# Attention heads beside a recurrence: one head a step where a unit of four was handled at once

## The chip, the cores and the metric

The kernel runs on one core of one Trainium2 chip. The metric is the device time of one execution in microseconds (us), the median of three runs. A core has TensorE (PE in the profile, its weight loads PEld), VectorE (DVE), ScalarE (ACT), GpSimd (POOL) and SyncE (SP), which issues the DMAs. Each engine works through its own list of instructions in order, and waits on semaphores that others raise.

## The reference

A decoder layer in float32 on 1024 rows of width 128. First come four sLSTM layers over 256 positions of 4 sequences. Each step of such a layer needs the state of the step before:

```python
raw = wx_t + jnp.einsum('bhd,hdgo->bhgo', h, rk) + b
mn = jnp.maximum(ir, lfm)
cn = fg * c + ig * jnp.tanh(zr)
nn = fg * n + ig
hn = jax.nn.sigmoid(og) * cn / nn
```

Each layer adds a feed-forward part, and layer norms follow. Then comes cross attention of 16 heads of 64 channels, from the 1024 rows to a context of 6404 rows of width 96: `softmax(q k^T / 8) v`, projected by Wo. Last come a layer norm, eight experts of which every token takes one, and a layer norm.

## The kernel before

**The recurrence.** `slstm_stage` runs the four layers as a wavefront: 38 chunks of 32 steps (`CH` = 32), 1216 steps in all. In a step, PE multiplies the state `st` by 16 recurrent matrices (L1325). ACT takes four activations of the sum, `tf`, `ei`, `tz`, `to` (L1176 to L1179). DVE makes the new state with nine short instructions, `uu` (L1478) first, then `rn`, `vv`, `ww`, `cn`, `hb`, and last the two parts of `st` (L1504, L1507); ACT copies a third part (L1185). PE may then start the next step. The position of a step in its chunk is called t below; at fixed t the engines also do the layers' other work (norms, convolution, gates, feed-forward), in the functions named `beside`.

**Plain chunks.** In the first 10 chunks the engines also prepare keys and values (`ByHead`: one tile of 512 columns at each t of its `PLACES`, copied by ACT at L1195) and fused weights (`WeightsByHead`). ACT scales six tiles of the context at t = `T_SCALE` (L1216), writes queries' weights at t = `T_QUERY` with two copies (L1223), and converts `wv_sb` once, in chunk 0 at t = `T_PARTS` (L1219); DVE makes the remainder of that one step later (L1523).

**Units.** In the other 28 chunks (896 steps) the attention of the first 512 rows runs beside the recurrence. A unit is 4 heads of one block of 128 rows; there are 16 units. Unit u starts at step 64 + 52 u (steps are counted from the first of the 28 chunks here). In each of its first 51 steps PE makes a tile of scores for 4 heads (L133, L135), ACT takes the exponential (L1165), and one step later PE multiplies by the values into `OA` (L1273). In the 52nd step there are no scores, and ACT copies `OA` to `o_sb` (L1169).

**Work around a unit.** Before a unit starts, its queries and, for each row, an upper value of its scores must be there. `Timetable` gives each piece its step:
- `queries`: PE multiplies `xat` by `qk_w` for 4 heads into one bank (L184), ACT copies it as two halves in the next two steps (L1145). For units from 2 on this is the last step of a unit.
- `head_queries`: the same with `wq_d`, 3 steps later (L192); ACT copies two halves (L1152), DVE subtracts and writes the low part 2 steps after (`dve_q_low`, L197).
- `maxes`: 52 pairs per unit, 13 pieces of keys by 4 heads. PE makes one piece of scores (`pe_max_score`, L144), DVE reduces it to its maximum (`dve_max`, L152). They are spread over the window of steps before the unit by the room on DVE: `ROOM` less `vector_load` at that t, less `special`.
- `column` and `row`: 4 and 3 steps before the unit, DVE reduces the 13 maxima of each head (L156), PE turns the 4 columns into rows (L162), ACT copies them (L1157).
- `out`: in the first step of the next unit, PE makes the 4 denominators (`pe_den`, L169), DVE takes the reciprocal (L1418), then PE projects 4 heads (`pe_project`, L176) and DVE adds them up (`dve_heads_out`, L207, L210).

**Two banks.** All these use two PSUM banks, `MB[0]` and `MB[1]`. `take` hands the bank that is read first to the next user, by the order of the steps; before PE writes a bank, `bank_for` waits until its last reader is done:

```python
def bank_for(key):
    bank, n = plan.uses[key]
    if n:
        pe.wait_ge(mb_read[bank], n)
```

**Order in a step.** PE: 16 recurrent matmuls, scores, values, bank work (`bank_work`: out, turn, queries, head queries, row, maxima), then `beside`. ACT: four activations, `beside_early`, `unit_early` (copies out of banks), the copy to `st`, `unit_late` (the exponential). DVE: the nine state instructions, `beside`, `unit_work` (block steps, out, low part, maxima, column).

After the recurrence, `attention_tail` does the other 512 rows and then the experts run; of these the change touches nothing that is computed.

## Time and profile before

| | |
|---|---|
| median of 3 runs | 4360.94 us (4358.36 to 4362.44) |
| the profiled execution | 4370.43 us |
| its span, first to last instruction | 4368.7 us |
| PE, DVE, ACT, POOL busy | 85%, 82%, 65%, 24% |
| recurrence, plain chunks | 56.9 to 867.5 us |
| recurrence, 28 chunks with units | 867.5 to 3225.9 us |
| tail and experts | 3225.9 to 4368.7 us |

PEclk, in 40 slices of the span: `6555555556999999999999999999978999999998`. A digit is the granted clock of TensorE in tenths of its full speed; the two levels are 1.0 (2.4 GHz) and 0.5 (1.2 GHz). A row of the windows view gives the busy time of each engine in a stretch with its number of instructions, and the mean granted clock. In the timeline a row gives the start, the duration, the engine, the line, what is written from what, how many instructions are merged, and in brackets how long the engine sat idle before it and what released it.

### The profile page before, as it was taken

Reading aid. Unit: us, or ns where it says so; the run is one execution under the profiler, and the core shown is the slowest. Engines: PE = TensorE matmul, PEld = TensorE weight load, DVE = VectorE, ACT = ScalarE, POOL = GpSimd, SP = SyncE. Lnnn points to the kernel's source line nnn. Section 1 sums busy time; section 2 is a strip of 40 time slices with the busy share of each in tenths; the row PEclk is TensorE's granted clock in tenths of the full one; section 3 lists DMA queues with packets and bytes.
Section 4 is the critical chain, followed back from the end, with each engine's and each line's share of the span. In section 5 each row is a group of like instructions: output and inputs, shape, how many; then the busy total and the mean of one; then the engine's idle time right before and its main releaser. Section 6 shows DMA issues by size and latency. Waiting matters only on the chain. (4 is left out here: it accounts for less than half of the span.)

```text
span 4368.7 us, 114098 instructions
## 1 busy us (share of the span) xinstructions
PE 3717.4 (85%) x42154; PEld 2230.8 (51%) x42154; DVE 3571.7 (82%) x16022; ACT 2839.8 (65%) x9118; POOL 1037.4 (24%) x1217
## 2 busy tenths in 40 slices
PE   5777777647998999999999999999868999999987
PEld 3433433434555555555555555555534555556555
DVE  7887788777888888888888888888758888888875
ACT  4555555544666666666666666666645888888884
POOL 1000000000000000000000000000005888889983
PEclk6555555556999999999999999999978999999998
DMA  3222222201333243343333333333333133322300
GB/s 100 67 68 70 66 70 71 75 16 24 74 81 76 66 89 73 73 88 72 70 81 73 78 70 81 80 73 83 80 87 93 48 78 78 78 55 63 78 25 25
DMA packets 262091, 305.39 MB, mean 70 GB/s; under 512 B 21752, under 2 KB 255032, under 8 KB 256376
## 3 DMA queue, kind: packets, MB, share of 16 engines
q1 hardware_dynamic: 258356, 293.73, 28.1%
q8 instruction: 332, 5.44, 0.6%
q10 hardware_dynamic: 3176, 4.36, 0.4%
q14 instruction: 227, 1.86, 0.2%
HBM read 241.03 MB, written 55.78 MB: 68 GB/s over the span
## 5 line engine op out<-in xcount | busy, mean ns | idle before, releaser
L1325 PEld LDWEIGHTS G<-st,rec_w 128*128 128x128 f16 x19456 | 604.2, 99 | 981.7 <-DVE st L1507 946.1
L1325 PE MATMUL G<-st,rec_w 128*128 128x1 f16 x19456 | 685.2, 165 | 354.9 <-DVE st L1507 341.0
L1779 POOL TENSOR_TENSOR plt<-pft,pht 128x512 f16<-128x512 f32 x765 | 867.2, 1166 | 156.0 <-DVE pht L2022 83.4
L1273 PE MATMUL OA<-pf,vals 128*97 128x512 f32 (+1 forms) x1632 | 877.7, 620 | 1.1
L1185 ACT ACTIVATE st<-hb 32x16 f16<-32x16 f32 x1216 | 258.8, 213 | 695.6 <-DVE hb L1502 695.2
L152 DVE TENSOR_REDUCE mx<-MB 128x1 f32<-128x512 f32 (+1 forms) x832 | 538.5, 661 | 56.2 <-PE MB L144 48.0
L1165 ACT ACTIVATE pf<-SC,ln_prob 128x512 f32<-128x512 f32 (+1 forms) x816 | 560.9, 687 | 20.5
L152 DVE TENSOR_REDUCE mx<-MT 128x1 f32<-128x512 f32 (+1 forms) x832 | 523.0, 663 | 54.1 <-PE MT L1828 44.1
L1774 ACT ACTIVATE pft<-ST,ln_prob 128x512 f32<-128x512 f32 (+1 forms) x816 | 537.4, 689 | 34.9 <-PE ST L1850 34.4
L1772 ACT ACTIVATE pht<-ST,ln_prob 128x512 f16<-128x512 f32 x510 | 351.5, 689 | 197.1 <-PE ST L1850 192.6
L135 PE MATMUL SC<-q_in,k_in 65*128 65x128 f16 (+1 forms) x3264 | 476.5, 223 | 0.0
L133 PE MATMUL SC<-qd_in,kc_in 128*128 128x128 f16 (+1 forms) x3264 | 472.1, 221 | 0.0
L1176 ACT ACTIVATE tf<-G 32x16 f32<-32x16 f32 x1216 | 213.0, 175 | 332.1 <-PE G L1325 301.6
L1478 DVE SCALAR_TENSOR_TENSOR uu<-tf,cn 32x32 f32<-32x32 f32 x1216 | 213.7, 176 | 236.0 <-ACT tf L1176 227.5
L769 POOL TENSOR_SCALAR vare<-yvar 128x4 f32<-128x4 f32 x39 | 7.6, 194 | 1550.3 <-DVE yvar L881 1550.3
L1912 PEld LDWEIGHTS OT<-vc,pht 128*128 128x128 f16 (+1 forms) x3264 | 251.4, 98 | 215.6 <-issue 17.3
L777 POOL TENSOR_SCALAR vare<-mv 128x1 f32<-128x1 f32 x78 | 15.0, 192 | 1393.6 <-DVE mv L787 1393.6
L1828 PE MATMUL MT<-kc,qd 128*128 128x512 f16 (+1 forms) x832 | 306.2, 389 | 43.0 <-DVE mx L152 41.0
L144 PE MATMUL MB<-keys_h,qh 96*128 96x512 f16 (+1 forms) x832 | 308.0, 394 | 31.4 <-DVE mx L152 28.3
L1912 PE MATMUL OT<-vc,pht 128*128 128x129 f16 (+1 forms) x3264 | 321.4, 221 | 9.9 <-DVE o_n L1978 6.6
L1484 DVE RECIPROCAL rn<-cn 32x16 f32<-32x16 f32 x1216 | 293.1, 241 | 41.9
L135 PEld LDWEIGHTS SC<-q_in,k_in 65*128 65x128 f16 (+1 forms) x3264 | 321.6, 99 | 0.0
(362 smaller groups left out, 7118.7 us busy)
## 6 DMA issues: line engine op xcount, KB each, us to landing
kc_in<-scr_k SPq DMA_DIRECT2D x384, 256.0 KB, 4.3
k_in<-scr_k SPq DMA_DIRECT2D x192, 256.0 KB, 4.9
vc<-scr_v SPq DMA_DIRECT2D x16, 1644.8 KB, 15.6
kc<-scr_k SPq DMA_DIRECT2D x32, 816.0 KB, 12.2
scr_v<-v_hl SPq DMA_DIRECT2D x24, 1032.0 KB, 5.5
scr_k<-k_hl SPq DMA_DIRECT2D x192, 128.0 KB, 1.7
k<-scr_k SPq DMA_DIRECT2D x16, 816.0 KB, 6.6
kc_in<-scr_k SPq DMA_DIRECT2D x32, 192.0 KB, 3.6
```

The costliest lines, as they stand in the source:

```text
L133: pe.matmul(bank[0:k, cols], at.kc_in[:, kept, i, first:first + k], at.qd_in[:, unit, cols], start=(i == 0), stop=False, skip_group_check= ...
L135: mm = pe.matmul(bank[0:k, cols], at.k2_in[:, kept, i, first:first + k], at.q2_in[:, unit, cols], start=False, stop=True, skip_group_check ...
L144: return pe.matmul(bank[:, 0:a1 - a0], at.qh[0:at.DC, unit, i * P:(i + 1) * P], at.keys_h[0:at.DC, a0:a1], start=True, stop=True)
L152: return at.nc.vector.tensor_reduce(at.mx[:, i, c:c + 1], bank[:, 0:a1 - a0], AX_X, ALU.max)
L1165: s.activation(pf[0:rows, tile % 2, :], SC[tile % 2][0:rows, :], ACT.Exp, scale=1.0 / at.S_SCALE, bias=at.ln_prob[0:rows, 0:1]).then_inc(p ...
L1273: pe.matmul(OA[0:at.DC + 1, :], at.vals[0:rows, i, :], pf[0:rows, tile % 2, :], start=(i == 0), stop=(i == KT - 1)).then_inc(pv_done, 1)
L1325: mm = pe.matmul(g[:, t, c:c + 1], rec_w[:, c, :], st[:, c:c + 1], start=False, stop=(c == C - 1), skip_group_check=True)
L1772: s.activation(ph[0:k, t % NP_, :], SC[t % NS][0:k, :], ACT.Exp, scale=1.0 / at.S_SCALE, bias=at.ln_prob[0:k, 0:1])
L1774: s.activation(pf[0:k, t % NP_, :], SC[t % NS][0:k, :], ACT.Exp, scale=1.0 / at.S_SCALE, bias=at.ln_prob[0:k, 0:1]).then_inc(p_done, 1)
L1779: return eng.tensor_tensor(pl[0:k, t % NP_, :], pf[0:k, t % NP_, :], ph[0:k, t % NP_, :], ALU.subtract)
L1828: pe.matmul(MB[done % 2][:, 0:a1 - a0], qd[:, h % NK_, i * P:(i + 1) * P], kc[:, h % NK_, a0:a1], start=True, stop=True).then_inc(m_done, 1)
L1912: pe.matmul(OA[i // 2][:, (i % 2) * 256:(i % 2) * 256 + VC], ph[0:k, t % NP_, i * P:(i + 1) * P], vc[0:k, g % 2, j, :], start=(j == 0 and ...
```

## The change

Queries, head queries, rows of maxima and the projection are done by single heads, one head in a step, each with a bank of its own. There are now 64 `queries`, 64 `head_queries`, 64 `column`, 64 `row` and 60 `out` steps, where there were 16, 16, 16, 16 and 15. A step takes at most one of `queries`, `head_queries`, `row`, `turn` and `out` (the set `taken`), `queries` and the head queries inside units only at t in `FOR_QUERIES`, `out` only at t in `FOR_OUT`. In a taken step at most one maximum is made, elsewhere at most four, but for the last step of a window. DVE reads `out` and head queries one step after PE, ACT copies queries, head queries and rows one step after PE. In the plain chunks `T_SCALE`, `T_QUERY` and `T_PARTS` move. The matmul for the denominator goes into column 128 of the bank that gets the projection of the same head. `tile_scores` waits at a unit's start for four banks of each kind in place of one, and the first piece of each head waits for that head's queries. The tail's own column of maxima keeps its old form. The core of the diff:

```diff
-def dve_max_column(at):
-    return at.nc.vector.tensor_reduce(at.mxn[:, :], at.mx[:, :, :], AX_X, ALU.max)
-def pe_max_row(pe, at, bank):
-    for i in range(at.HEADS_A_UNIT):
-        mm = pe.matmul(bank[at.DHEAD:at.DHEAD + 1, i * P:(i + 1) * P], at.mxn[:, i:i + 1], at.identa[:, :], start=True, stop=True)
-    return mm
+def dve_max_column(at, i):
+    return at.nc.vector.tensor_reduce(at.mxn[:, i:i + 1], at.mx[:, i, :], AX_X, ALU.max)
+def pe_max_row(pe, at, bank, i):
+    return pe.matmul(bank[at.DHEAD:at.DHEAD + 1, 0:P], at.mxn[:, i:i + 1], at.identa[:, :], start=True, stop=True)
 
...
-def pe_queries(pe, at, bank, unit):
-    for i in range(at.HEADS_A_UNIT):
-        mm = pe.matmul(bank[0:at.DC, i * P:(i + 1) * P], at.qk_w[:, unit * at.HEADS_A_UNIT + i, :], at.xat[:, :],
-                       start=True, stop=True)
-    return mm
...
+def pe_out(pe, at, bank, unit, i):
+    cols = slice(i * P, (i + 1) * P)
+    pe.matmul(bank[:, P:P + 1], at.o_sb[:, cols], at.pick_den[:, :], start=True, stop=True)
+    return pe.matmul(bank[:, 0:P], at.o_sb[0:at.DC, cols], at.vo_w[:, unit * at.HEADS_A_UNIT + i, :], start=True, stop=True)
+def pe_queries(pe, at, bank, unit, i):
+    return pe.matmul(bank[0:at.DC, 0:P], at.qk_w[:, unit * at.HEADS_A_UNIT + i, :], at.xat[:, :], start=True, stop=True)
...
+    FOR_QUERIES = (0, 1, 2, 3, 5, 6, 7, 11, 12, 15, 18, 19, 20)
+    FOR_OUT = (1, 2, 4, 7, 8, 14, 15, 18, 21, 27, 31)
...
-        self.out = {start[u] + period: u for u in range(units - 1)}
...
-        self.queries = {35: 0, 46: 1}
-        self.queries.update({start[v - 2] - 1: v for v in range(2, units)})
-        self.head_queries = {s + 3: v for s, v in self.queries.items()}
-        self.column = {start[v] - 4: v for v in range(units)}
-        self.row = {start[v] - 3: v for v in range(units)}
-        asked = {v: s for s, v in self.queries.items()}
-        special = {s: 1.3 for s in self.out}
-        special.update({s: 0.6 for s in self.column})
+        H = range(at.HEADS_A_UNIT)
+        taken = set(self.turn)
+        def next_free(places, s):
+            while s % chunk_steps not in places or s in taken:
+                s += 1
+            taken.add(s)
+            return s
+        self.queries, self.head_queries, self.out, self.column, self.row = {}, {}, {}, {}, {}
+        asked = {}
+        asked[0] = 34
+        for i in H:
+            self.queries[next_free(range(chunk_steps), 34 + i)] = 0, i
+        for i in H:
+            self.head_queries[next_free(range(chunk_steps), 40 + 5 * i)] = 0, i
+        for i in H:
+            s = next_free(self.FOR_QUERIES, start[0] + 1 + i)
+            self.queries[s] = 1, i
+            asked.setdefault(1, s)
+        for i in H:
+            self.head_queries[next_free(range(chunk_steps), start[0] + 22 + 5 * i)] = 1, i
+        for u in range(units):
+            for i in H:
+                if u:
+                    self.out[next_free(self.FOR_OUT, start[u] + 2 + 10 * i)] = u - 1, i
+            if u + 2 < units:
+                for i in H:
+                    s = next_free(self.FOR_QUERIES, start[u] + 1 + 4 * i)
+                    self.queries[s] = u + 2, i
+                    asked.setdefault(u + 2, s)
+                for i in H:
+                    s = next_free(self.FOR_QUERIES, start[u] + 17 + 5 * i)
+                    assert s < start[u + 1] - 5
+                    self.head_queries[s] = u + 2, i
...
+        special = {s + 1: 0.55 for s in self.out}
-            special[s + 2] = special.get(s + 2, 0.0) + 0.7
+            special[s + 1] = special.get(s + 1, 0.0) + 0.25
...
+                if s != window[-1]:
+                    upto = min(upto, n + (1 if s in taken else 4))
                 if upto > n:
                     self.maxes.setdefault(s, []).extend((v, i) for i in range(n, upto))
                 n = upto
+            for i in H:
+                last = max(s for s in window if (v, (i + 1) * len(at.KEYS) - 1) in self.maxes.get(s, ()))
+                self.column[last + 1] = v, i
+                s = last + 2
+                while s in taken or len(self.maxes.get(s, ())) > 1:
+                    s += 1
+                assert s < start[v] - 1
+                taken.add(s)
+                self.row[s] = v, i
...
-                take(("den", self.out[s]), s + 0.5)
-                take(("out", self.out[s]), s + 0.6)
+                take(("out",) + self.out[s], s + 1.7)
-                take(("queries", self.queries[s]), s + 2.3)
+                take(("queries",) + self.queries[s], s + 1.3)
             if s in self.head_queries:
-                take(("head queries", self.head_queries[s]), s + 2.5)
+                take(("head queries",) + self.head_queries[s], s + 1.7)
             if s in self.row:
-                take(("row", self.row[s]), s + 1.3)
+                take(("row",) + self.row[s], s + 1.3)
...
-    T_SCALE, SCALE_TILES, T_QUERY, T_PARTS = 16, 6, 27, 26
+    T_SCALE, SCALE_TILES, T_QUERY, T_PARTS = 9, 6, 29, 30
...
+                        if step - 1 in plan.queries:
+                            v, i = plan.queries[step - 1]
+                            bank, n = plan.uses["queries", v, i]
+                            a.wait_ge(mb_full[bank], n + 1)
+                            s.activation(at.qh[0:at.DC, v % at.UNITS_A_BLOCK, i * P:(i + 1) * P], MB[bank][0:at.DC, 0:P],
+                                         ACT.Copy).then_inc(mb_read[bank], 1)
+                        if step - 1 in plan.head_queries:
+                            v, i = plan.head_queries[step - 1]
+                            bank, n = plan.uses["head queries", v, i]
+                            a.wait_ge(mb_full[bank], n + 1)
+                            s.activation(at.qd_in[:, v % at.UNITS_A_BLOCK, i * P:(i + 1) * P], MB[bank][:, 0:P],
+                                         ACT.Copy).then_inc(hq_hi, 1)
...
-                            u = plan.out[step]
+                            u, i = plan.out[step]
                             pe.wait_ge(o_kept, u + 1)
-                            bank, full = bank_for(("den", u))
-                            pe_den(pe, at, bank).then_inc(full, 1)
-                            bank, full = bank_for(("out", u))
-                            pe_project(pe, at, bank, u % at.UNITS_A_BLOCK).then_inc(full, 1)
+                            bank, full = bank_for(("out", u, i))
+                            pe_out(pe, at, bank, u % at.UNITS_A_BLOCK, i).then_inc(full, 1)
...
-                        if step in plan.out:
-                            u = plan.out[step]
-                            bank, n = plan.uses["den", u]
+                        if step - 1 in plan.out:
+                            u, i = plan.out[step - 1]
+                            done = at.HEADS_A_UNIT * u + i
+                            bank, n = plan.uses["out", u, i]
                             dve.wait_ge(mb_full[bank], n + 1)
-                            v.reciprocal(at.rden[:, :], MB[bank][:, 0:at.HEADS_A_UNIT]).then_inc(mb_read[bank], 1)
-                            dve.wait_ge(mb_read[bank], n + 1)
-                            bank, n = plan.uses["out", u]
-                            dve.wait_ge(mb_full[bank], n + 1)
-                            dve_heads_out(dve, at, MB[bank], at.y_unit[:, u + 1, :], y_step, (at.HEADS_A_UNIT - 1) * u,
-                                          mb_read[bank])
-                        if step - 2 in plan.head_queries:
-                            q = plan.head_queries[step - 2]
-                            bank, n = plan.uses["head queries", q]
-                            dve.wait_ge(hq_hi, 2 * (q + 1))
-                            dve_q_low(at, MB[bank], q % at.UNITS_A_BLOCK).then_inc(mb_read[bank], 1)
+                            v.reciprocal(at.rden[:, i:i + 1], MB[bank][:, P:P + 1]).then_inc(den_ready, 1)
+                            dve.wait_ge(den_ready, done + 1)
+                            y, head = at.y_unit[:, u + 1, :], MB[bank][:, 0:P]
+                            if i == 0:
+                                v.tensor_scalar(y, head, at.rden[:, 0:1], None, ALU.mult).then_inc(mb_read[bank], 1)
+                            else:
+                                last_bank, last = plan.uses["out", u, i - 1]
+                                dve.wait_ge(mb_read[last_bank], last + 1)
+                                v.scalar_tensor_tensor(out=y, in0=head, scalar=at.rden[:, i:i + 1], in1=y,
+                                                       op0=ALU.mult, op1=ALU.add).then_inc(mb_read[bank], 1)
+                        if step - 1 in plan.head_queries:
+                            q, i = plan.head_queries[step - 1]
+                            bank, n = plan.uses["head queries", q, i]
+                            dve.wait_ge(hq_hi, plan.head_queries_done[q, i])
+                            dve_q_low(at, MB[bank], q % at.UNITS_A_BLOCK, i).then_inc(mb_read[bank], 1)
```

## Rows read from the trace of the kernel before

**Rows 1.** Windows: stretch, us, busy (count) of PE, PEld, DVE, ACT, POOL, PEclk, DMA.

```profile
867.50:1054.70 187.20, 98.72 (x1255) 64.35 (x1256) 141.61 (x739) 68.91 (x352) 8.52 (x24) 0.50 0.08 16
1054.70:3225.90 2171.20, 1977.63 (x24423) 1205.03 (x24421) 1840.73 (x9640) 1445.56 (x5352) 95.59 (x272) 0.97 0.36 76
```

**Rows 2.** Timeline of a step with no maximum, from state to state.

```profile
2043.19 0.17 DVE L1507 TENSOR_TENSOR st<-hb,st 32x16 f16<-32x16 f32 x1
...
2043.42 0.55 PE L1325 MATMUL G<-st,rec_w 128*128 128x1 f16 x16 [0.39 <-DVE st L1507]
...
2044.06 0.17 ACT L1176 ACTIVATE tf<-G 32x16 f32<-32x16 f32 x1
...
2044.27 0.18 DVE L1478 SCALAR_TENSOR_TENSOR uu<-tf,cn 32x32 f32<-32x32 f32 x1
...
2045.74 0.55 PE L1325 MATMUL G<-st,rec_w 128*128 128x1 f16 x16 [0.39 <-DVE st L1507]
```

**Rows 3.** Timeline of steps with one maximum and with two.

```profile
1989.88 1.28 DVE L152 TENSOR_REDUCE mx<-MB 128x1 f32<-128x512 f32 x2
...
1990.35 0.17 ACT L1176 ACTIVATE tf<-G 32x16 f32<-32x16 f32 x1
...
1991.08 0.17 DVE L1478 SCALAR_TENSOR_TENSOR uu<-tf,cn 32x32 f32<-32x32 f32 x1
```

**Rows 4.** Timeline, PE's first recurrent matmul after a step with one maximum.

```profile
2048.12 0.55 PE L1325 MATMUL G<-st,rec_w 128*128 128x1 f16 x16 [0.24 <-DVE st L1507]
```

**Rows 5.** Windows: steps 3 to 48 of each unit; the last unit, and the sum.

```profile
3111.10:3218.60 107.50, 95.32 (x1296) 57.75 (x1294) 75.71 (x489) 78.97 (x294) 4.61 (x14) 1.00 0.36 75
sum 1837.80, PE 1663.74 PEld 988.90 DVE 1614.50 ACT 1263.32 POOL 84.03; mean PE 103.98 PEld 61.81 DVE 100.91 ACT 78.96 POOL 5.25
```

**Rows 6.** Windows: the six steps around each of 15 unit ends; two, and the sum.

```profile
1592.30:1610.20 17.90, 17.12 (x214) 11.64 (x212) 14.26 (x73) 11.40 (x43) 0.00 (x0) 1.00 0.07 14
...
2136.30:2162.40 26.10, 25.04 (x211) 18.00 (x209) 14.67 (x71) 10.81 (x39) 0.00 (x0) 0.67 0.17 35
...
sum 314.80, PE 297.42 PEld 205.44 DVE 215.06 ACT 171.93 POOL 11.56; mean PE 19.83 PEld 13.70 DVE 14.34 ACT 11.46 POOL 0.77
```

**Rows 7.** Timeline around the unit end at 2010 us.

```profile
2003.58 0.39 PE L144 MATMUL MB<-keys_h,qh 96*128 96x512 f16 x1 [0.79 <-DVE mx L152]
...
2008.40 1.11 PE L184 MATMUL MB<-xat,qk_w 128*96 128x128 f32 x8
...
2010.61 1.02 PE L169 MATMUL MB<-pick_den,o_sb 97*128 97x1 f32 x8
...
2012.66 2.07 PE L176 MATMUL MB<-vo_w,o_sb 96*128 96x128 f32 x8 [1.03 <-DVE rden L1418]
```

**Rows 8.** Timeline, the rows of another unit at the full clock.

```profile
2277.93 1.03 PE L162 MATMUL MB<-identa,mxn 128*1 128x128 f32 x8
```

**Rows 9.** Groups by line, DVE, 1054.7 to 3225.9: name, shapes, count, busy us, mean ns, idle.

```profile
L210 DVE SCALAR_TENSOR_TENSOR y_unit<-MB,rden,y_unit 128x128 f32<-128x128 f32 x45 | 15.8, 351 | 1.6
...
L197 DVE TENSOR_TENSOR q_in<-MB,qd_in 64x512 f16<-64x512 f32 x14 | 9.4, 668 | 0.1
...
L943 DVE TENSOR_TENSOR x<-TP,x 128x128 f32<-128x128 f32 x26 | 7.6, 292 | 0.8
...
L156 DVE TENSOR_REDUCE mxn<-mx 128x4 f32<-128x52 f32 x15 | 2.9, 194 | 0.4 <-issue 0.3
L1418 DVE RECIPROCAL rden<-MB 128x4 f32<-128x4 f32 x15 | 2.7, 180 | 3.5 <-PE MB L169 3.4
```

**Rows 10.** Timeline of plain steps at t = 16, then t = 27, ScalarE.

```profile
261.70 0.60 ACT L1195 ACTIVATE k_hl<-SC 128x512 f16<-128x512 f32 x1 [0.43 <-DMA scr_k<-k_hl]
262.20 0.68 ACT L1216 ACTIVATE vals<-vals 128x576 f32<-128x576 f32 x1
...
372.14 0.60 ACT L1195 ACTIVATE k_hl<-SC 128x512 f16<-128x512 f32 x1 [1.02 <-PE SC L1345]
...
372.64 0.50 ACT L1223 ACTIVATE wq_d<-wq_sb 128x128 f32<-128x128 f32 x2
```

More of the change, by code:

```diff
@@ L292, in __init__ @@
                 n = upto
+            for i in H:
[7 more added lines that the diff above has]
+                self.row[s] = v, i
+            assert n == at.MX
+        for tile in self.queries.values():
+            asked_at = next(s for s, key in self.queries.items() if key == tile)
+            assert asked_at < min(s for s, keys in self.maxes.items() if (tile[0], tile[1] * len(at.KEYS)) in keys)
         self.uses, free, count = {}, [-1.0, -1.0], [0, 0]
@@ L1256, in tile_scores @@
                             for kind in ("head queries", "row"):
-                                bank, n = plan.uses[kind, u]
-                                pe.wait_ge(mb_read[bank], n + 1)
+                                for head in range(at.HEADS_A_UNIT):
+                                    bank, n = plan.uses[kind, u, head]
+                                    pe.wait_ge(mb_read[bank], n + 1)
                             if u == 0:
@@ L1433, in unit_work @@
                         if step in plan.column:
-                            u = plan.column[step]
+                            u, head = plan.column[step]
                             for bank in range(2):
-                                n = max(n for (kind, *key), (b, n) in plan.uses.items() if kind == "max" and key[0] == u and b == bank)
-                                dve.wait_ge(mb_read[bank], n + 1)
-                            dve_max_column(at).then_inc(m_col, 1)
+                                n = max((n for (kind, *key), (b, n) in plan.uses.items()
+                                         if kind == "max" and key[0] == u and key[1] // len(at.KEYS) == head and b == bank), default=-1)
+                                if n >= 0:
+                                    dve.wait_ge(mb_read[bank], n + 1)
+                            dve_max_column(at, head).then_inc(m_col, 1)
                     def dve_renew(t, c, k):
```

68 lines of the change are left out of this document (27 added, 41 removed).

## The prediction, made before the changed kernel was run

> **What bounds the kernel now.** I read the page first, then windows by stage, then timelines of single steps, and last windows cut at the unit ends. The change touches only the recurrence, 56.9 to 3225.9 us. There no engine's mean load decides, but the loop from state to state. In a step without extras TensorE's recurrent matmuls start at 2043.42 and the next ones at 2045.74: 2.32 us [rows 2]. Two engines can lengthen it. VectorE is done with the state at 2043.19 + 0.17 = 2043.36 and starts `uu` at 2044.27, so what it does in between costs nothing up to 0.91 us. TensorE sits idle for 0.39 us before the next matmuls; with one maximum 0.24 us is left [rows 2, 4]. Two maxima take VectorE 1.28 us, and `uu` starts 0.73 us after `tf` where 0.21 is normal: 0.5 us late [rows 2, 3].
>
> The 832 steps with units take 2171.2 us [rows 1]. At 2.32 each they would take 1930.2; 241 us is excess. The windows divide it. Steps 3 to 48 of all units, 736 steps, take 1837.8 us, 2.50 each [rows 5]. The six steps around each of 15 unit ends, 90 steps, take 314.8 us, 3.50 each [rows 6]. The first 64 steps, in which unit 0 has its 52 maxima squeezed into some 24 steps, take 187.2 us against 148.5 [rows 1]: 39 us excess.
>
> Why a unit end is long: rows of maxima for four heads hold TensorE about 1.0 us, queries about 1.1 [rows 7, 8], in steps whose slack is 0.2 to 0.4. At `out` the projection waits for VectorE's reciprocal, which stands behind the state in VectorE's queue (TensorE idle 1.03 us), and VectorE then needs 4 x 0.351 us [rows 7, 9]. Part of the length is the clock: the end at 1592 has 1.00 throughout and takes 17.9 us, the one at 2136 has a mean of 0.67 and takes 26.1 [rows 6]. A mean of 0.67 is two thirds of the stretch (17.2 us) at 1.2 GHz, and 8.2 us dearer: 0.48 us a us. Over all 15 ends it is about 0.40. The mean of 0.97 over 2171 us [rows 1] is 130 us at the lower level, so some 52 us of time.
>
> **What the change removes.** No unit end has batches of four any more. If its six steps cost what interior steps of units 0 to 14 cost, (1837.8 - 107.5) / 690 = 2.51 us [rows 5], 90 steps take 226 us: 89 us go. But the work comes back elsewhere, and it is priced for all 832 steps at once.
>
> **Maxima by steps.** In the trace before I counted the interior steps by their maxima and read for each the time from state to `uu` beyond 0.91. 155 steps with none are 0.03 us long, 467 with one 0.15, 114 with two 0.45 (half of [rows 3]'s case falls where other VectorE work is small). Check: 5 + 70 + 51 = 126 us, and the windows give 1837.8 - 736 x 2.32 = 130 [rows 5]. Working the new `Timetable` through gives 197 steps with none, 491 with one, 143 with two, one with three: 6 + 74 + 64 + 1 = 145 us.
>
> **What the single heads add.** From the same timetable:
> - TensorE, at full clock, a quarter of the batches: 0.24 to 0.28 for queries, row and denominator, as much for the projection, so about 0.5 for `out` [rows 7, 8]. Beside a maximum, queries and row just fill the 0.24 left: 0.03 each, about 100 steps, 3 us. `out` with a maximum: 52 steps, 0.2 each, 10 us.
> - VectorE for one head of the low part: 64x512 takes 0.668, 128x128 from PSUM 0.292 [rows 9], so 0.29. For one head of `out`: 0.18 + 0.35 and a wait between, 0.58. In steps with one maximum and no bank wait (9 and 16 of them) I take 0.2 and 0.25: 6 us. A column costs about 0.15 (four heads take 0.194), felt in 28 steps with maxima: 4 us.
> - **A new wait.** VectorE reads `out` and the head queries one step after TensorE, so their bank stays held. In 48 of the 832 steps TensorE needs a second bank in just that step (91 has head queries and a maximum, 92 a row and a maximum); before, 20 steps were so. TensorE's maximum then waits behind VectorE's state and its read, and behind it in TensorE's queue stand `beside` and the next recurrent matmuls. VectorE, from the end of the state: read 0.29, semaphore 0.05, the matmul 0.39 [rows 7], maximum 0.66, other work about 0.3: 1.7 against 0.91, some 0.8 long where 0.15 to 0.45 is charged already. I add 0.6: 29 us. Bounds: 0.2 (10 us), if the other work falls into the wait, and 1.0 (48 us) behind an `out`; [rows 7] shows 0.79 us of idle for a wait of this kind.
>
> ScalarE's copies are one of 128 columns in place of two of 256, one step later, and lie in its gap between `to` and the `st` copy; cost 0, and up to 0.1 us in steps where a norm also stands there (at most 10 us in all). The eight waits at a unit's start are for steps at least three earlier. No DMA, and no place in SP's or POOL's list, moves.
>
> Adders: 3 + 10 + 6 + 4 + 29 = 52 us, bounds 30 to 85.
>
> **The clock.** The last step of a unit keeps its missing scores and the first its missing values, so TensorE is still little loaded there, but the long waits are gone. I take half of the 130 us at the lower level, 65 x 0.40 = 26 us; bounds 0 and 52.
>
> So 832 steps: 1930 + 145 + 52 + 26 = 2153 us against 2171: -18. The first 64 steps keep batches of four and five maxima (7 steps with three or more, before 10): -2, bounds -10 and +6.
>
> **The weight copies.** At t = 16 the scale of 0.68 us starts at 262.20, inside the key copy that ends at 262.30, and runs to 262.88, where `tf` follows. Without it `tf` could start 0.58 earlier; 8 chunks: 4.6 us. At t = 27 the key copy ends at 372.74, the two query copies at 373.14: 0.40, 8 chunks, 3.2 us [rows 10]. At t = 9 and 29 no key copy stands in the slot, and in the later chunks the exponentials fit into it. T_PARTS acts once; I take 0 (bounds -1 and +1). Sum -8, bounds -10 and -3.
>
> **Two rules of the Trainium skill.** The 128-wide operation at 0.292 us and the 512-wide one at 0.668 [rows 9] leave 0.17 us that does not depend on width. "VectorE: DVE Perf Modes", section on the TRN2 errata, says that every instruction pays such a fixed part and advises tiles of 512 elements or more, against this change. Ten more VectorE instructions a unit (3 low parts, 3 reciprocals, 3 columns) at about 0.17 would be 25 us if all of it were in the loop. By my sum only what exceeds the 0.91 counts. The granted clock falls at unit ends in which TensorE shows 25.0 us busy of 26.1 [rows 6]. "TensorE: Matmul & The Clock Gate", Part 1, ties the lower level to an idle TensorE; going by idleness alone the time at 1.2 GHz would be gone, which is the rival below.
>
> **Sum.** -18 - 2 - 8 = -28 us on the profiled execution (4370.4 us, span 4368.7). The median of the runs shown is 4360.94, 9 us less; I take the same difference: 4333 us.
>
> **Rivals.**
> - More gain: the clock never falls (-26), or the bank waits hide behind VectorE's other work (-29). Either gives about -55: 4306. For it: four of 15 ends stay at 1.00 already. Against: a unit's last and first step keep their small load.
> - No net change: the clock falls as long as before (+26): -2, 4359. For it: falls come also away from unit ends, after steps with idle TensorE, and 48 bank waits make more such steps.
> - Slower, one mechanism: each bank wait leaves TensorE without work and the clock falls for a step behind it. A step at 1.2 GHz costs 2.5 x 0.48 = 1.2 us; 48 of them are 58, less the 10 taken for falls there already: +48, so +20 and 4381. It decides from 31 of 48 on: 28 + 9 us are needed.
> - The work is not spread: heads crowd in neighbouring steps since the allowed t are few (head queries of unit 4 at 193, 194, 195). It would show as the second rival; its part in the 48 is counted.
>
> **Chances.** Forecast 0.52 (own range 4318 to 4348), more gain 0.22, no net change 0.15, slower 0.11. A measurement can tell 0.2%, 8.7 us. Faster: 0.52 and 0.22, 0.74; within 0.15; slower 0.11. Range 4302 to 4360: it takes in the larger gain and most of the third case.
>
> **What would show it.** Six-step windows around unit ends near 15 to 17 us in place of 21. Interior steps up from 2.50 to about 2.58. TensorE waiting for `q_in` or `y_unit` of VectorE before L144's matmuls, some 48 times. A mean clock of 0.98 or more in the units. In the plain chunks `tf` 0.4 to 0.6 us earlier after t = 16 and 27. Wrong would be: bank waits of over 1.3 us each, interiors above 2.62, a clock at 0.96 or less, or new ScalarE delay of the `st` copy.

## The result, and the profile after

The changed kernel takes 4332.73 us, the median of 5 runs (4330.71 to 4336.2), where the kernel before took 4360.94 (5 runs, 4349.77 to 4362.44): ratio over all runs 0.9949, 95% interval 0.9937 to 0.9960. It is faster by 0.5%; the two medians alone are 28.2 us apart (0.65%). The prediction was 4333 us, with 4302 to 4360 as range.

Windows of the kernel after, columns as in [rows 1]: the plain chunks, the first 64 steps of the others, the steps with units. Before, the last two took 187.20 and 2171.20 us [rows 1].

```profile
56.85:861.90 805.05, 600.32 (x6470) 316.59 (x6468) 645.59 (x3567) 476.62 (x1990) 34.71 (x100) 0.50 0.21 69
861.90:1036.24 174.34, 93.39 (x1226) 58.30 (x1227) 137.55 (x740) 68.96 (x356) 8.42 (x24) 0.50 0.08 17
1036.24:3188.68 2152.44, 1970.13 (x24446) 1208.08 (x24447) 1847.19 (x9769) 1469.86 (x5456) 95.12 (x272) 0.97 0.36 77
```

Both kernels cut at the same events (each step's `tf`) give the table: 37.7 us of span are gone.

| us | before | after | difference | predicted |
|---|---|---|---|---|
| plain chunks | 810.7 | 805.1 | -5.6 | -8 |
| first 64 steps | 187.2 | 174.3 | -12.9 | -2 |
| 831 steps with units | 2168.8 | 2152.4 | -16.4 | -18 |
| tail and experts | 1145.2 | 1142.3 | -2.9 | 0 |

The profiled execution of the kernel before (4370.43 us) is 9.5 us above its median, and that of the kernel after is its median; so the column of differences sums to 37.8 us where the medians differ by 28.2. The tail isn't touched by the change; it spreads over 1141.5 to 1146.2 us in the kernels measured here.

Windows after of six steps around the unit ends (two, and the sum of 15), then of steps 3 to 48 of the units (the last, and the sum), which answer to [rows 5, 6]:

```profile
1571.04:1589.88 18.84, 18.38 (x180) 10.37 (x178) 13.67 (x70) 10.45 (x40) 0.00 (x0) 0.70 0.06 14
...
2927.64:2942.83 15.19, 13.45 (x162) 8.14 (x159) 13.30 (x76) 11.16 (x42) 1.07 (x4) 0.89 0.66 122
...
sum 251.60, PE 234.15 PEld 139.59 DVE 201.97 ACT 159.50 POOL 11.61; mean PE 15.61 PEld 9.31 DVE 13.46 ACT 10.63 POOL 0.77
...
3075.44:3183.80 108.36, 96.70 (x1310) 59.49 (x1308) 77.09 (x497) 79.35 (x294) 4.60 (x14) 1.00 0.34 74
sum 1887.81, PE 1723.70 PEld 1059.42 DVE 1637.82 ACT 1302.05 POOL 83.52; mean PE 107.73 PEld 66.21 DVE 102.36 ACT 81.38 POOL 5.22
```

An end takes 16.8 us in place of 21.0, 63 us less for 15; an interior step takes 1887.8 / 736 = 2.565 in place of 2.497, 50 us more in all. The shortest end has a clock of 0.89 and the longest 0.70: all 15 still lose the clock for a while, where four of 15 did not before.

**The new wait, in a timeline** of the kernel after (start, us, engine, line; in brackets the idle time and its end). Head queries stand in two steps in a row here:

```profile
1123.65 0.16 DVE L1553 TENSOR_TENSOR st<-hb,st 32x16 f16<-32x16 f32 x1
...
1124.12 0.28 DVE L195 TENSOR_TENSOR q_in<-MB,qd_in 64x128 f16<-64x128 f32 x1
...
1124.46 0.39 PE L144 MATMUL MB<-keys_h,qh 96*128 96x512 f16 x1 [0.77 <-DVE q_in L195]
...
1124.69 0.54 PE L1364 MATMUL G<-st,rec_w 128*128 128x1 f16 x16
1124.89 0.69 DVE L152 TENSOR_REDUCE mx<-MB 128x1 f32<-128x512 f32 x1 [0.48 <-PE MB L144]
...
1125.27 0.18 ACT L1216 ACTIVATE tf<-G 32x16 f32<-32x16 f32 x1 [0.78 <-PE G L1364]
...
1125.50 0.17 DVE L1524 SCALAR_TENSOR_TENSOR uu<-tf,cn 32x32 f32<-32x32 f32 x1
```

The state is done at 1123.81, but TensorE's recurrent matmuls start at 1124.69 and not at 1123.87: they stand behind a maximum (L144) that waits for the bank that VectorE's low part (L195) frees at 1124.40. From state to `uu` it is 1.69 us, 0.78 over the floor of 0.91. The groups of the stretch with units count such waits; the first row is of the kernel before, the second of the one after:

```profile
L144 PE MATMUL MB<-keys_h,qh 96*128 96x512 f16 x776 | 275.7, 380 | 5.5 <-DVE mx L152 5.5
```

```profile
L144 PE MATMUL MB<-keys_h,qh 96*128 96x512 f16 x780 | 277.3, 383 | 41.2 <-DVE q_in L195 21.0 <-DVE y_unit L1466 16.0 <-DVE mx L152 4.2
```

**Where the clock falls** in the kernel after, in windows of the first and second step of a unit and the first recurrent matmuls of the second:

```profile
1986.83:1989.46 2.63, 1.49 (x28) 1.17 (x29) 2.42 (x14) 1.61 (x7) 0.00 (x0) 0.74 0.13 21
1989.46:1993.33 3.87, 3.87 (x31) 2.04 (x30) 3.16 (x14) 1.61 (x7) 0.00 (x0) 0.50 0.02 4
```

```profile
1988.81 0.59 PE L1364 MATMUL G<-st,rec_w 128*128 128x1 f16 x16 [1.13 <-DVE st L1553]
...
1990.07 1.97 PE L1314 MATMUL OA<-pf,vals 128*97 128x512 f32 x2
```

The first step of a unit has no values to multiply, and TensorE is idle for 1.13 us of it. Within that idle time its clock goes to 1.2 GHz: the mean granted clock is 0.98 from 1987.50 to 1988.10 and 0.50 from 1988.10 to 1988.80. The values of the second step take 1.97 us, and it takes 3.87 us.

### The profile page after: what moved, and what is told of

It reads as the page before. It is cut to its first block and busy times, and to the rows that moved or that the text cites. A ratio compares the mean times of both kernels' runs of the same rounds, so it can differ in the third digit from the quotient of the medians.

```text
span 4331.0 us, 114618 instructions
## 1 busy us (share of the span) xinstructions
PE 3704.3 (86%) x42154; PEld 2228.9 (51%) x42154; DVE 3573.7 (83%) x16163; ACT 2871.1 (66%) x9230; POOL 1036.1 (24%) x1217
## 5 line engine op out<-in xcount | busy, mean ns | idle before, releaser
L1205 ACT ACTIVATE pf<-SC,ln_prob 128x512 f32<-128x512 f32 (+1 forms) x816 | 562.3, 689 | 20.6
L1958 PEld LDWEIGHTS OT<-vc,pht 128*128 128x128 f16 (+1 forms) x3264 | 251.2, 98 | 215.1 <-issue 16.4
L144 PE MATMUL MB<-keys_h,qh 96*128 96x512 f16 (+1 forms) x832 | 306.7, 396 | 60.3 <-DVE q_in L195 22.9
## 6 DMA issues: line engine op xcount, KB each, us to landing
kc<-scr_k SPq DMA_DIRECT2D x32, 816.0 KB, 12.9
```

The source lines that it names most:

```text
L144: return pe.matmul(bank[:, 0:a1 - a0], at.qh[0:at.DC, unit, i * P:(i + 1) * P], at.keys_h[0:at.DC, a0:a1], start=True, stop=True)
L1205: s.activation(pf[0:rows, tile % 2, :], SC[tile % 2][0:rows, :], ACT.Exp, scale=1.0 / at.S_SCALE, bias=at.ln_prob[0:rows, 0:1]).then_inc(p ...
L1958: pe.matmul(OA[i // 2][:, (i % 2) * 256:(i % 2) * 256 + VC], ph[0:k, t % NP_, i * P:(i + 1) * P], vc[0:k, g % 2, j, :], start=(j == 0 and ...
```

## The experiments

These measures are used in the text. "Low" is TensorE's time at 1.2 GHz in the steps with units. "Full excess" and "low excess" are the sums of the time from state to `uu` beyond 0.91 us, over the steps at the full clock and over those that touch a stretch at the lower one. They come from the profiled execution alone; the ratio comes from 4 to 11 runs and has the last word. "Ends" counts the unit ends, of the 15 six-step windows, with a mean granted clock of 1.00. "Clock" is the mean granted clock of whole executions, the lowest and the highest of that kernel's runs. e1 to e4, e5 to e8 and e9 to e12 are three groups, each with its own runs of the kernel before.

| kernel | ratio to before (95%) | units, us | low | full excess | low excess | ends | clock |
|---|---|---|---|---|---|---|---|
| before | 1 | 2168.8 | 135 | 154.5 | 81.5 | 4 | 0.852 to 0.860 |
| after | 0.9949 (0.9937 to 0.9960) | 2152.4 | 129 | 181.5 | 42.2 | 0 | 0.854 to 0.857 |
| e1 weights only | 0.9987 (0.9977 to 0.9997) | 2161.9 | 114 | 165.5 | 66.6 | 3 | 0.856 to 0.860 |
| e2 no bank wait | 0.9917 (0.9903 to 0.9931) | 2140.9 | 142 | 157.7 | 53.5 | 0 | 0.853 to 0.856 |
| e3 clock filled | 0.9942 (0.9926 to 0.9958) | 2141.4 | 63 | 186.8 | 25.0 | 13 | 0.858 to 0.864 |
| e4 out batch | 0.9965 (0.9952 to 0.9978) | 2158.2 | 147 | 159.1 | 69.2 | 0 | 0.852 to 0.855 |
| e5 changed again | 0.9959 (0.9946 to 0.9971) | 2163.6 | 154 | 178.2 | 56.1 | 0 | 0.852 to 0.855 |
| e6 rows batch | 0.9930 (0.9918 to 0.9942) | 2149.4 | 116 | 178.4 | 41.4 | 0 | 0.856 to 0.859 |
| e7 queries batch | 0.9903 (0.9888 to 0.9919) | 2128.5 | 54 | 178.8 | 20.6 | 8 | 0.863 to 0.864 |
| e8 no wait, filled | 0.9876 (0.9862 to 0.9890) | 2126.8 | 79 | 165.9 | 31.6 | 7 | 0.859 to 0.862 |
| e9 = e7 again | 0.9909 (0.9896 to 0.9923) | 2134.7 | 64 | 176.7 | 26.3 | 9 | 0.860 to 0.862 |
| e10 query batch moved | 0.9967 (0.9954 to 0.9979) | 2162.6 | 132 | 175.1 | 55.7 | 0 | 0.855 to 0.856 |
| e11 out only | 0.9926 (0.9912 to 0.9939) | 2145.9 | 96 | 174.5 | 39.0 | 9 | 0.857 to 0.862 |
| e12 batch, filled | 0.9887 (0.9874 to 0.9901) | 2125.6 | 48 | 172.8 | 20.9 | 11 | 0.862 to 0.866 |

**e1: the weight copies alone** (kernel before otherwise).

```diff
-    T_SCALE, SCALE_TILES, T_QUERY, T_PARTS = 16, 6, 27, 26
+    T_SCALE, SCALE_TILES, T_QUERY, T_PARTS = 9, 6, 29, 30
```

> The kernel before with only the three times of the weight copies moved (t = 16, 27, 26 to 9, 29, 30). Theory (from the changed kernel's plain chunks, 805.1 us against 810.7): the copies' steps win 5.1 us at t = 16, and at t = 27 and 28 together nothing, since TensorE's tile of step 27 is late by its own work; so -5 to -6 us. Rival (my prediction's step): both win, -8 us. A second rival: the plain chunks gain nothing when measured alone, 0 us, and the 5.6 are from elsewhere.

Measured 0.9987, by that ratio 5.7 us less (the medians differ by 4.0); the plain chunks take 805.1 us, as in the kernel after. Step by step, the kernel after against the kernel before (e1 gives the same within 0.2 us): the ten steps t = 16 are 5.1 us shorter, t = 26 0.7, and t = 27 2.35; but t = 28 is 2.75 longer and t = 30 0.4. T_QUERY wins nothing. The timeline after at t = 27 and 28 shows why:

```profile
370.39 0.60 ACT L1235 ACTIVATE k_hl<-SC 128x512 f16<-128x512 f32 x1 [1.02 <-PE SC L1384]
...
371.01 0.18 ACT L1216 ACTIVATE tf<-G 32x16 f32<-32x16 f32 x1
...
372.46 0.16 DVE L1553 TENSOR_TENSOR st<-hb,st 32x16 f16<-32x16 f32 x1
372.54 0.63 PE L1384 MATMUL SC<-keys_h,wk_h 96*128 96x512 f16 x1
...
372.97 0.21 PE L1364 MATMUL G<-st,rec_w 128*128 128x1 f16 x1
```

`tf` follows the key copy at once, as predicted, and the step is 0.38 shorter; the state is done at 372.62. But TensorE, at 1.2 GHz here, is still at its own key tile (L1384) and starts the next step at 372.97, 0.3 late. What one step gains the next one loses.

**e2: the bank waits taken away.** Maxima keep out of the steps in which VectorE reads `out` or head queries, where these would need a second bank; 7 such waits remain, in steps with three or four maxima.

```diff
+        held = {s + 1 for s in (*self.out, *self.head_queries)}
-                    upto = min(upto, n + (1 if s in taken else 4))
+                    upto = min(upto, n + (4 - 3 * (s in taken or s in held) - (s in taken and s in held)))
```

> The changed kernel, but in a step in which VectorE still has to read a projection or head queries at most one maximum is made, and none if that step also holds queries, head queries, a row or a projection. Steps in which TensorE must wait for a bank behind VectorE fall from 48 to 7 of 832; for it, 5 steps get three maxima and 2 get four. Theory: a bank wait costs about 0.7 us more than a plain step with one maximum (measured excess 0.91 against 0.17 to 0.25), so 41 x 0.7 = -29 us, less 10 for the crowded steps: -18 us (-10 to -25) against the changed kernel. Rival: VectorE's own load in these steps is what costs, the wait lies beneath it, and the load only moves: 0 us, up to +5.

0.9917: 14 us less than the change by the ratios (0.9949 - 0.9917 = 0.0032), within the 10 to 25 expected. In its trace the full excess falls from 181.5 to 157.7, 24 us, while low excess rises by 11. The waits are worth that 24 us: 48 of them cost 0.907 us each in the kernel after, 43.5 in all, of which the maxima in those steps would have cost 12 anyway; and seven steps at full clock that now have three or four maxima take 10 us of excess.

**e3: the clock held up at unit ends.** Two matmuls of 512 columns in the last step of a unit and four in the first, whose result nobody reads; what is computed stays as it was.

```diff
+                                for _ in range(n):
+                                    pe.matmul(SC[(tile + (first == 0)) % 2][:, 0:512], at.qh[0:at.DC, u % at.UNITS_A_BLOCK, 0:P],
+                                              at.keys_h[0:at.DC, 0:512], start=True, stop=True)
```

> The changed kernel with 2 more float16 matmuls of 512 columns in the last step of a unit (where scores are missing) and 4 in the first of the next (where values are missing), into a bank of scores that nobody reads; results are unchanged. Theory: TensorE's small load in these two steps is what lets the clock fall at 14 of 15 unit ends; filled, the time at 1.2 GHz in the units falls from 129 us to 40 or less, and at the 0.23 us a us that the changed kernel shows that is -20 us (-12 to -28). Rival 1: the price is the 0.40 of my prediction: -36 us. Rival 2: the falls stem from other steps and stay: 0 us.

The trace has 63 us at the lower level in place of 129, unit ends of 15.5 us (232.3 / 15), and 13 of 15 ends at the full clock where the kernel after has none. The clock is higher in every execution: the six have 0.858 to 0.864, the ten of the changed kernel (with e5) 0.852 to 0.857. But the trace is of the fastest of the six (4324.3); four of them, at 0.858 to 0.860, took 4335.0 to 4342.8, and the median, 4335.2, is not below the change's. The expected 20 us did not come, and the ratio can't tell e3 from the change: that filling lowers the time is not shown by this run. e8 bears on it.

**e4: `out` in one batch again**, the rest as changed.

```diff
-            for i in H:
-                if u:
-                    self.out[next_free(self.FOR_OUT, start[u] + 2 + 10 * i)] = u - 1, i
+        self.out = {start[u] + period: u for u in range(units - 1)}
```

> The changed kernel with denominators and projections as before: four heads at once in the first step of the next unit, DVE reading them in that step. Theory: the unit end waits twice for VectorE there and is dearer by about 35 us over 15 ends, while 52 steps with a head's projection (0.1 each) and 18 held banks (0.7) are saved, about 18: +15 to +22 us against the changed kernel. Rival: the projection's batch was the whole length of the unit ends, since queries and rows fit beside it: +40 us or more.

0.9965, 7 us more than the change; unit ends 278.7 in place of 251.6, interiors 1866.4 in place of 1887.8. That is less than the 15 to 22 us expected, and the two intervals overlap: what `out` by heads is worth beside the other single heads is not shown by this run. e11 says more.

**e5: the changed kernel once more.**

> The changed kernel itself, on the same chip as the other experiments of this call, as the control for their differences. Both theories expect the ratio measured first, 0.9949 (0.9937 to 0.9960), 4336 us; a time outside 4328 to 4344 would say that the differences between calls are larger than the effects of the parts.

4345.07 against 4362.21, ratio 0.9959; so the change is faster again, but by 17 us where it was 28; the time is 12 us above the first one and just outside the 4328 to 4344 that were named. Its trace has 154 us at the lower level where the other had 129, and 14 us more of low excess: the same program loses the clock for different times. That is the size below which differences between groups of runs aren't to be read here.

**e6: columns and rows in batches again**, and **e7: queries and head queries in batches again**, each with the rest as changed, in one group with e5.

```diff
-            for i in H:
-                last = max(s for s in window if (v, (i + 1) * len(at.KEYS) - 1) in self.maxes.get(s, ()))
...
+        self.column = {start[v] - 4: v for v in range(units)}
+        self.row = {start[v] - 3: v for v in range(units)}
```

> The changed kernel with columns and rows of maxima as before: one column reduction 4 steps and four row matmuls 3 steps before a unit. Theory: the batch made step 49 of a unit about 1.0 us long, 15 us in all; spread, rows cost 0.1 in 31 steps, 0.7 in the 7 to 9 with a held bank and columns 0.1 in 28, about 12 us. So +3 us (0 to +8) against the changed kernel: nearly nothing. Rival: the unit ends' gain is shared evenly by the three kinds of batch: +10 to +15 us.

```diff
+        self.queries = {35: 0, 46: 1}
+        self.queries.update({start[v - 2] - 1: v for v in range(2, units)})
+        self.head_queries = {s + 3: v for s, v in self.queries.items()}
```

> The changed kernel with queries and head queries as before: four heads in the last step of a unit and three steps later, two half copies each, VectorE's low part two steps after. Theory: the two batches made steps 51 and 2 long by 12 and 19 us in all and brought some of the first 64 steps' 13 us; spread, 30 bank waits at 0.7 take 21 back. So +8 to +15 us against the changed kernel, part of it in the first 64 steps. Rival: the batches cost more than the spread work in every kind alike: +20 us or more; second rival: the bank waits eat the whole, 0 or less.

e6 is 14 us faster than e5, e7 25 us (0.9903 against 0.9959), where both were expected to be slower. I had held that batches cost; that fell. e6's gain lies in the low excess (41.4 in place of 56.1), with the full excess the same; its interval overlaps that of the first measurement of the change. The batch takes 40 of the 48 bank waits with it (8 are left), and yet the full excess is the same as e5's, 178.8 against 178.2: the batches cost at full clock about what the waits did. What differs is the lower clock: 54 us in place of 154, low excess 20.6 in place of 56.1. Two theories were left: fewer waits, or the batch's place, the last step of a unit, in which scores are missing.

**e8: e2 and e3 together** (its diff is the two).

> Both edits at once: no bank waits (4321 us measured alone, 15 us below the changed kernel) and the filled steps at the unit ends (in its profiled execution 11 us below the changed kernel in the units, in the median of its runs nothing). Theory: the fills win what the clock costs at unit ends, some 0.17 to 0.23 us a us, but runs differ by when the clock falls, so a median of 4310 to 4320. Rival: filling wins nothing that lasts, 4321 or above.

0.9876, 4306.97 us: 38 us below e5 in the same group, and against the change 26 by the medians and 32 by the ratios; the fastest kernel here, faster than e2 and e3, and below the 4310 to 4320 expected. Full excess 165.9, low excess 31.6. From e2 it differs by the filled matmuls alone: the ratio falls from 0.9917 to 0.9876, 18 us, with intervals that don't overlap, though the two were measured in different groups; the ends at the full clock go from none to 7 and the low excess from 53.5 to 31.6. This is the best evidence here that filling lowers the time.

**e9 and e10: the batch's place.** e9 is e7 again; e10 moves one number.

> The kernel with queries and head queries in batches of four and all else as changed, once more, as the base of this group. Ratio to before 0.990 as measured (0.9888 to 0.9919); TensorE at 1.2 GHz in the units for 45 to 75 us.

```diff
-        self.queries.update({start[v - 2] - 1: v for v in range(2, units)})
+        self.queries.update({start[v - 2] + 2: v for v in range(2, units)})
```

> One number differs from the base of this group: the batch of queries stands in a unit's third step in place of its last one (the head queries three steps behind it as before). Theory: what made the batch cheap is that it gives TensorE work in the step without scores, so that the clock doesn't fall at the unit end. Then the time at 1.2 GHz goes from 50 us back to 100 to 140, and the kernel is 15 to 30 us slower than the base (steps with a bank wait go from 8 to 19, of which 7 us). Rival: the gain came from the 40 bank waits that are gone; then the time at 1.2 GHz stays at 45 to 75 us and the kernel is 5 to 10 us slower than the base.

e10 is 25 us slower than e9 (4350.32 against 4325.58) and all of it is the clock: low 132 in place of 64, low excess 55.7 in place of 26.3, full excess unchanged, no end at the full clock in place of 9, and 0.855 or 0.856 in all five executions against 0.860 to 0.862 in e9's four. The same unit end in windows of single steps, the last step of a unit, the first and the second, with the recurrent matmuls that end the idle time of the first; e9, then e10:

```profile
1984.58:1987.25 2.67, 2.67 (x31) 1.75 (x31) 2.23 (x12) 1.82 (x7) 0.00 (x0) 1.00 1.04 208
1987.25:1989.58 2.33, 1.40 (x29) 1.01 (x27) 2.12 (x13) 1.99 (x7) 0.00 (x0) 1.00 0.00 0
1989.58:1992.24 2.66, 2.36 (x31) 1.27 (x29) 2.45 (x14) 1.99 (x7) 0.00 (x0) 1.00 0.00 0
```

```profile
1988.94 0.55 PE L1351 MATMUL G<-st,rec_w 128*128 128x1 f16 x16 [0.93 <-DVE st L1542]
```

```profile
1994.20:1996.47 2.27, 1.90 (x23) 0.82 (x24) 1.85 (x12) 1.82 (x7) 0.00 (x0) 1.00 1.12 230
1996.47:1999.10 2.63, 1.32 (x28) 0.98 (x26) 2.42 (x13) 1.61 (x7) 0.00 (x0) 0.97 0.10 16
1999.10:2002.89 3.79, 3.79 (x32) 1.97 (x30) 3.17 (x14) 1.60 (x7) 0.00 (x0) 0.57 0.02 4
```

```profile
1998.45 0.55 PE L1351 MATMUL G<-st,rec_w 128*128 128x1 f16 x16 [1.31 <-DVE st L1542]
```

With the batch TensorE is busy for all 2.67 us of the last step, and the clock holds through a first step with 0.93 us idle. Without it the last step is a light one (1.90 us busy of 2.27), the first has 1.31 us idle, and the second runs at 1.2 GHz: 3.79 us in place of 2.66. The theory of the waits allowed 5 to 10 us and 75 us of low clock; it falls. The fuller last step and the shorter idle time of the first come together here, and no run parts them.

**e11: only `out` by heads.** Columns and rows are in a batch too (both diffs above, with e9).

> Only the projection is by single heads; queries, head queries, columns and rows are in batches of four as before the change; the new places of the weight copies stay. Theory: the gain of the change is that of `out` and of the weight copies, and the rest costs as much as it gives. Then 0 to 8 us faster than the base of this group, ratio to before 0.988 to 0.990. Rival: the row of maxima in a batch holds TensorE 1.0 us in one step near the unit end, 0.8 more than its slack, 15 times: then 8 to 15 us slower than the base.

4335.54, 10 us slower than e9, with queries in batches in both. The theory falls. The rival's size fits, its mechanism doesn't: full excess is 174.5, less than e9's 176.7, and the whole difference lies in low excess, 39.0 in place of 26.3. With the queries single (e6, e5) the sign was the other way. Both are differences in the clock; what rows as such cost is below them. Against the kernel before, e11 is as fast as the whole change or faster (0.9926; the change 0.9949 and 0.9959): of the five kinds of work that were split, `out` alone, with the weight copies, gives as much as all five, while e4, with the other four, gives 15 us. 9 of e11's 15 ends keep the full clock where the kernel before has 4 and e1 has 3, all with the batch of queries in the last step. This points to the batch of `out` with its wait as one more thing that let the clock fall.

**e12: e9, filled in the first step and without bank waits behind `out`.**

```diff
+        held = {s + 1 for s in self.out}
+                                for _ in range(4):
+                                    pe.matmul(SC[(tile + 1) % 2][:, 0:512], at.qh[0:at.DC, u % at.UNITS_A_BLOCK, 0:P],
+                                              at.keys_h[0:at.DC, 0:512], start=True, stop=True)
```

> Queries in batches as in the base of this group, no maximum two at a time in the steps where VectorE still reads `out` (the bank waits behind it go, 8), and four matmuls of 512 columns whose result nobody reads in the first step of every unit, where the values are missing. Results are the same. Theory: the last step is kept busy by the queries' batch and the first by the added matmuls, so the time at 1.2 GHz goes from 50 to 10 to 35 us: worth 4 to 12 us, and the waits 4 to 7; 8 to 18 us faster than the base, ratio to before 0.986 to 0.988. Rival: the added matmuls hold TensorE 1.6 us in a step that they lengthen as much as the low clock did: then within 4 us of the base.

4315.17, 10 us faster than e9, in the range of the theory; full excess is 4 lower, low excess 5. Two edits stand in it, and the part of each is not shown: 11 ends at the full clock against 9, and 48 us of low clock against 64, are a difference of the size that e7 and e9, one program, show (8 and 9, 54 and 64). The four matmuls stand in the idle time of the first step (row of that step: 2.18 us busy of 2.34, in e9 1.40 of 2.33) and don't lengthen it:

```profile
1985.23:1987.57 2.34, 2.18 (x34) 1.33 (x32) 2.13 (x13) 1.98 (x8) 0.00 (x0) 1.00 0.01 1
```

## Why the prediction was right

**The total** came out to the microsecond, and part of that is luck. By the medians 28.2 us are gone; e1 puts 4 to 6 of them to the weight copies and the windows 12.9 to the first 64 steps, which leaves some 10 for the steps with units, where 18 were predicted. The traces say how loose that is: the same steps with units took 2168.8 us in the kernel before and 2161.9 in e1, and 2152.4 and 2163.6 in two executions of the kernel after, so they gained between 16 us and nothing. The error there and the one in the first 64 steps cancelled. The shape was right: 63 us less at the unit ends, 50 more in the interiors.

**The floor and the maxima** held. Plain steps in the trace after are 0.02, 0.17 and 0.44 us long for none, one and two maxima, predicted from before as 0.03, 0.15, 0.45; over the timetable's counts that is 151 us where 145 stood.

**The adders** were predicted at 52 us. At full clock, with some 12 us for what the steps at the lower clock would have cost, the excess is 194, less 151: 43. The bank wait was sized right. By the timetable there are 48; the view of L144's idle times, us and number, has 47 that VectorE's low part and `out` end:

```profile
  DVE q_in L195: 22.9, 30
...
  DVE y_unit L1466: 16.0, 17
```

Each such step costs 0.907 us, 32 us beyond the maxima in it, predicted 29. The small adders were put at 23 and cost 11: `out` on TensorE beside a maximum adds 0.06 (0.23 in place of 0.17), not 0.2, while a row adds 0.11 and not 0.03. VectorE's single heads take what the groups of the kernel after show:

```profile
L195 DVE TENSOR_TENSOR q_in<-MB,qd_in 64x128 f16<-64x128 f32 x60 | 16.3, 272 | 0.6
L1466 DVE SCALAR_TENSOR_TENSOR y_unit<-MB,rden,y_unit 128x128 f32<-128x128 f32 x45 | 15.8, 351 | 1.6
L1458 DVE RECIPROCAL rden<-MB 128x1 f32<-128x1 f32 x60 | 9.3, 154 | 0.7
L156 DVE TENSOR_REDUCE mxn<-mx 128x1 f32<-128x13 f32 x60 | 9.2, 154 | 0.1
```

A column of 13 takes 154 ns and one of 52 took 194, a reciprocal of one 154 where four took 180 [rows 9]. The width hardly counts in such small instructions. "VectorE: DVE Perf Modes", on the TRN2 errata, of the Trainium skill puts this down to a fixed cost per instruction, and these rows agree. The 25 us that I worked out from it (it is nine instructions more a unit, not ten) did not reach the path: all adders but the waits are 11.

**The clock** is the step whose reasons were wrong and whose number came out. I took 65 us at the lower level by 0.40. The trace has 129 us, for 42.2 - 12 = 30 us: twice the time at little over half the price, 0.23. Reckoned the same way, e5 gives 0.28 (56.1 less 13 for the steps as such, over 154). The likely reason, not tested, is that TensorE has less to do in those steps, and so more slack, once the batches are gone. The time is as long as before because I named the wrong cause, or half of it: the batches and long waits of a unit end. e10 shows that the batch of queries held the clock up, and e3 and e8 that it holds more often when the thin last and first steps are filled; the batch of `out` with its wait did seem to let it fall (e11). I had read "25.0 us busy of 26.1" [rows 6] as a busy TensorE losing its clock, but two thirds of that row is time at the lower level, where matmuls take nearly twice as long (1.97 us for values that take 1.05). "TensorE: Matmul & The Clock Gate", Part 1, of the Trainium skill ties the lower level to an idle TensorE; the single steps agree with that (a step with 1.13 or 1.31 us idle, and the fall in or just after it) better than my reading did. Idleness in one step alone doesn't separate all of them: 0.93 us after a full step did no harm, and the same step of two executions, with 1.75 us idle, kept the clock in one and lost it in the other (below).

**The first 64 steps** were outside my bounds: -12.9, not -2 (-10 to +6). The step that failed was counting only the steps with three or more maxima, and not the batches of queries. All of it runs at 1.2 GHz [rows 1], where the batch of queries takes TensorE 2.00 us (at 987.54 in the kernel before) and not 1.11. The windows divide it: with all in batches but `out`, 180.7 (e11), so 6 come from the new places of the maxima; with single rows 181.0 (e9); with single queries 174.3: 6.7 us from these.

**The weight copies** gave -5.6 of -8: t = 16 was right (-5.1 over nine chunks, predicted -4.6 over eight), t = 27 wrong, as e1 shows; "what is late next" was asked of ScalarE and not of TensorE.

**The signs I named.** Unit ends 16.8 (predicted 15 to 17), interiors 2.565 (2.58), 48 waits: right. A mean clock of 0.98 or more: wrong, 0.97. `tf` earlier after t = 27: seen, and worth nothing. The rivals: the condition of "no net change", a clock that falls for as long as before, did come true (129 us; 135 before, 114 in e1); it cost 30 us and not 52, and the first 64 steps gave 11 more than counted. The slower one, the clock falling behind each bank wait, happened at one wait of 48, the one at which TensorE is idle longest:

```profile
2718.17 0.39 PE L144 MATMUL MB<-keys_h,qh 96*128 96x512 f16 x1 [1.75 <-DVE mx L152]
```

The second maximum of this step waits until VectorE has read the first, behind two instructions of a norm and the low part of head queries. The mean granted clock is 1.00 from 2715.00 to 2718.50, with TensorE busy for 1.75 us of 3.50, and 0.50 from 2718.50 to 2721.00. A second such wait (1.75 us idle before 1637.38) kept the clock in this trace and lost it in e5's. "More gain" did not come for this kernel; with the waits gone and the clock held, by other edits, e8 reaches 4307.

What stays open: why the time at 1.2 GHz of one and the same program is 129 us in one execution and 154 in another, and why e3 with a higher clock in all its executions is in the median no faster than the change, while e8 is faster than e2.

## What to carry to other kernels

Where a shared buffer is freed one step later, count the steps in which the next user needs it: here 48 such waits cost 32 us, more than all other overhead of splitting the work (11); and split one kind of work at a time, since `out` alone brought as much as all five kinds together (e11). Work that fills a step may be what keeps TensorE's clock up in its thin neighbours (the batch of queries did, e10): before it is spread, look at single-step windows of busy time and granted clock on either side. And when a late engine is relieved, ask which engine is late next by a hair; the gain at t = 27 went there.

## What was not expected of the hardware

- At a unit end the granted clock fell to 1.2 GHz in or just after steps with 1.13 and 1.31 us of idle TensorE behind a light step, and held with 0.93 us behind a full one. No idle time of TensorE in the steps with units of the kernel after is longer than 1.75 us, and yet all 15 ends lose the clock.
- Six matmuls without use in the last and first step of a unit held the clock at 13 of 15 ends (e3) where none held it; without bank waits they went with 18 us less (e8 against e2).
- A microsecond at 1.2 GHz cost 0.40 us in steps with batches, and 0.23 and 0.28 in two executions without.
- The same program spent 129 and 154 us at 1.2 GHz in two executions, in this part alone.
